# Moving the decay-matrix loads from SyncE's queue to ScalarE's, with the orders around them, in a Mamba2 block kernel

## The reference

```python
x = layernorm(x + attn(x)); x = layernorm(x + ffn(x))       # x: 2 x 512 x 512
# attn: a Mamba2 block, 128 heads of 64, state 128, 8 groups, chunks of 128 tokens
proj = einsum('bsd,ed->bse', x, in_proj_w)                  # gate | hs, B, C | dt
hBC = silu(conv1d(proj[hs, B, C], 4 taps) + conv_b)
dt = clip(softplus(dt + dt_bias), 0, 100); A_cum = cumsum(dt * -exp(A_log)) in each chunk
L = exp(segsum(dt * A))                                     # exp(A_cum[l] - A_cum[s]), l >= s
Y_diag = einsum('bzlhn,bzshn,bhzls,bzshp->bzlhp', C, B, L, hs * dt)
Y_off = C @ (state carried from the chunks before) * exp(A_cum)
g = (Y_diag + Y_off + hs * D) * silu(gate)
out = g * rsqrt(mean(g * g in each group) + eps) * norm_w
return out @ out_proj_w.T
# ffn: x @ W.T + bias plus the weighted sum of 8 low-rank products
```

## Time and profile before

| | us |
|---|---|
| median of 3 runs (lowest to highest) | 1553.58 (1553.01 to 1557.14) |
| the profiled execution's own time | 1554.98 |
| its span in the trace | 1553.1 |
| PE busy | 1522.9 (98%) |
| DVE, POOL, ACT busy | 1350.6 (87%), 1340.1 (86%), 1219.3 (79%) |

### The profile page before, as it was taken

How to read it: one execution, slowest core, us unless ns; L and a number is a source line. 1 busy time by engine, 2 the same in 40 slices (tenths; PEclk the granted TensorE clock), 3 DMA queues, 4 the chain that set the end, 5 groups by cost and what they waited for, 6 DMA issues and landing times.

```text
span 1553.1 us, 27611 instructions
## 1 busy us (share of the span) xinstructions
PE 1522.9 (98%) x8664; PEld 1260.5 (81%) x8664; DVE 1350.6 (87%) x1878; ACT 1219.3 (79%) x2360; POOL 1340.1 (86%) x1124
## 2 busy tenths in 40 slices
PE   8899999999999999999999999999999999999998
PEld 6778888878888888888888788888888888888765
DVE  6678799888989899897998979988898979989797
ACT  5888877888778887788868886888877888788863
POOL 4489989899889988899899998899988997989974
PEclk9999999999999999999999999999999999999999
DMA  3654643545345543635436454454534444363521
GB/s 114 224 181 142 191 143 120 168 143 168 111 144 173 153 147 117 193 120 158 157 118 187 127 161 143 128 182 133 171 108 162 155 141 154 123 192 121 177 89 61
DMA packets 164192, 229.06 MB, mean 147 GB/s; under 512 B 25040, under 2 KB 86480, under 8 KB 163792
## 3 DMA queue, kind: packets, MB, share of 16 engines
q1 hardware_dynamic: 163040, 227.14, 46.3%
q10 hardware_dynamic: 1008, 0.17, 0.1%
HBM read 193.14 MB, written 34.08 MB: 146 GB/s over the span
## 4 chain that ended last, share of the span: by engine, by line
PE 56%; POOL 23%; issue 10%; DVE 7%; ACT 2%; DMA 2%; SPq 0%; POOLq 0%; DVEq 0%; ACTq 0%
PE proj L665 10%; PE proj L667 10%; PE proj L666 10%; PE p_out L714 4%; PE p_out L716 4%; PE p_out L715 4%; POOL w_lo L1340 4%; POOL dh L1398 4%; PE p_st L723 3%; POOL dh L1422 3%; POOL xd_lo L1383 2%; POOL y L1443 2%; POOL xdt L1365 2%; PE p_yd L832 2%; POOL xd L1372 2%
## 5 line engine op out<-in xcount | busy, mean ns | idle before, releaser
L665 PE MATMUL proj<-x_hi,w_hi 128*128 128x512 f32 x1160 | 465.8, 402 | 7.7 <-DVE x_lo L1824 7.3
L667 PE MATMUL proj<-x_hi,w_lo 128*128 128x512 f32 x1160 | 453.9, 391 | 0.0
L666 PE MATMUL proj<-x_lo,w_hi 128*128 128x512 f32 x1160 | 453.7, 391 | 0.0
L1340 POOL TENSOR_TENSOR w_lo<-raw,w_hi 128x512 fp32r<-128x512 f32 x177 | 249.2, 1408 | 87.2 <-ACT w_hi L923 86.2
L1681 DVE SCALAR_TENSOR_TENSOR hs<-proj,uch,hs 128x511 f32<-128x511 f32 (+2 forms) x384 | 283.9, 744 | 44.1 <-ACT hs L949 38.1
L1011 ACT ACTIVATE decay<-decay,tok 128x128 f32<-128x128 f32 x1024 | 312.5, 390 | 2.5 <-DMA decay<-acum_d 2.3
L665 PEld LDWEIGHTS proj<-x_hi,w_hi 128*128 128x128 f32 x1160 | 219.6, 189 | 51.0 <-issue 9.4
L667 PEld LDWEIGHTS proj<-x_hi,w_lo 128*128 128x128 f32 x1160 | 218.7, 189 | 47.1
L666 PEld LDWEIGHTS proj<-x_lo,w_hi 128*128 128x128 f32 x1160 | 219.5, 189 | 41.7
L1443 POOL TENSOR_TENSOR y<-y,gate 128x512 f32<-128x512 f32 x128 | 193.6, 1512 | 34.2 <-DVE y L1862 25.7
L714 PE MATMUL p_out<-wo_hi,g_hi 128*128 128x512 f32 x512 | 202.5, 395 | 3.2 <-DVE g_lo L1750 2.7
(11 more groups left out here) (142 smaller groups left out, 2980.1 us busy)
## 6 DMA issues: line engine op xcount, KB each, us to landing
decay<-acum_d SPq DMA_DIRECT2D x128, 512.0 KB, 4.5
raw<-w_t SPq DMA_DIRECT2D x177, 256.0 KB, 3.6
turned_d<-x_tok_sb SPq DMA_DIRECT2D x112, 256.0 KB, 3.9
x_tok_sb<-turned_d SPq DMA_DIRECT2D x448, 64.0 KB, 1.9
eac<-eacum_d SPq DMA_DIRECT2D x192, 128.0 KB, 3.0
wo_raw<-wo_t SPq DMA_DIRECT2D x64, 256.0 KB, 4.6
hs<-x_t SPq DMA_DIRECT2D x8, 256.0 KB, 6.0
acc<-x_tok SPq DMA_DIRECT2D x8, 256.0 KB, 3.2
```

What stands on the lines that cost most here:

```text
L665: nc.tensor.matmul(dst[:], w_hi[:, ws, k, :], x_hi[:, k, cols], start=(k == 0), stop=False)
L666: nc.tensor.matmul(dst[:], w_hi[:, ws, k, :], x_lo[:, k, cols], start=False, stop=False)
L667: mm = nc.tensor.matmul(dst[:], w_lo[:, ws, k, :], x_hi[:, k, cols], start=False, stop=(k == KC - 1))
L1340: nc.gpsimd.tensor_tensor(w_lo[:, s].rearrange("p a b -> p (a b)"), raw[:, s, :], w_hi[:, s].rearrange("p a b -> p (a b)").bitcast(F32), A ...
```

## The change

124 of the 128 decay loads are issued by ACT, at fixed places between its other calls; the four of the prologue stay on SP. SP waits at two more places, before it loads a later unit's channel constants, until `skip` of the unit's last step is done. The matmul engine's order is as before. On ACT, DVE and POOL calls change places:

```diff
@@ SP: every load_decay goes (16 in a group), as in
-                load_decay(sp, g, 0, 4)
...
                 load_eac(sp, g, 0, 2)
-                load_decay(sp, g, 0, 5)
                 store_blocks(g, 0, 4)
                 load_w(g, STEP_TILES[0][4][0])
...
                 if not last:
+                    sp.wait_ge(dskip_done, carried(g, 0, 7))
                     load_channels(sp, 2 * g + 2, 0)
                     load_unit(sp, 2 * g + 2, 0)
@@ ACT, first_unit
                 exps(g, 0, 2)
                 gaps(g, 0, 3)
                 squares(g, 0, 0)
+                wo_split_hi(g, 0, (0,))
+                load_decay(act, g, 0, 4)
                 exps(g, 0, 3)
-                wo_split_hi(g, 0, (0,))
                 wo_split_hi(g, 0, (1,))
                 split_hi(g, STEP_TILES[0][1][1])
                 wo_split_hi(g, 0, (2,))
                 wo_split_hi(g, 0, (3,))
+                split_hi(g, STEP_TILES[0][2][0])
                 high_gated(step(g, 0, 0))
                 drain_proj(g, STEP_TILES[0][0][1], (0,))
-                split_hi(g, STEP_TILES[0][2][0])
                 gaps(g, 0, 4)
                 split_hi(g, STEP_TILES[0][3][0])
                 drain_proj(g, STEP_TILES[0][1][0], (0,))
                 drain_proj(g, STEP_TILES[0][1][1], (0,))
+                load_decay(act, g, 0, 5)
                 high_gated(step(g, 0, 1))
                 exps(g, 0, 4)
-                save_half(g, 0)
                 squares(g, 0, 1)
                 drain_proj(g, STEP_TILES[0][2][0], (0,))
+                save_half(g, 0)
...
@@ ACT, last_unit
                         exps(g, 1, c + 3)
+                    if c < 4:
+                        load_decay(act, g, 1, c + 4)
                     squares(g, 1, c)
@@ POOL, first_unit
-                split_lo(g, STEP_TILES[0][1][0])
-                skip(g, 0, 1)
                 decayed_tokens(g, 0, 1)
                 gate_y(g, 0, 0)
+                skip(g, 0, 1)
                 high_tokens(g, 0, 1)
                 scale_tokens(g, 0, 2)
                 low_tokens(g, 0, 1)
+                split_lo(g, STEP_TILES[0][1][0])
                 if g:
                     inv_rms(g - 1, 6)
                 split_lo(g, STEP_TILES[0][1][1])
+                add_carried(g, 0, 1)
+                decay_state(g, 0, 1)
                 split_lo(g, STEP_TILES[0][2][0])
-                decay_state(g, 0, 1)
-                add_carried(g, 0, 1)
@@ DVE, first_unit
+                state_sum(g, 0, 0)
                 turn_blocks(g, 0, 3)
                 high_tokens(g, 2)
-                state_sum(g, 0, 0)
...
-                turn_blocks(g, 0, 6)
                 square_sum(g, 0, 2)
                 tap(g, STEP_TILES[0][3][0], 0, 1)
                 tap(g, STEP_TILES[0][3][0], 0, 2)
                 tap(g, STEP_TILES[0][3][0], 0, 3)
+                turn_blocks(g, 0, 6)
```

More of the change, by code:

```diff
@@ L635, in body @@
                     load_w(g + 1, STEP_TILES[0][1][1])
+                if not last:
+                    sp.wait_ge(dskip_done, carried(g, 1, 7))
                     load_channels(sp, 2 * g + 3, 1)
@@ L1154, in first_unit @@
                 drain_proj(g, STEP_TILES[0][3][0], (1,))
+                save_half(g, 2)
                 high_gated(step(g, 0, 3))
                 squares(g, 0, 3)
+                gaps(g, 0, 7)
                 drain_proj(g, STEP_TILES[0][4][0], (0,))
-                gaps(g, 0, 7)
                 silus(g, [STEP_TILES[0][3][0]], (1,))
-                save_half(g, 2)
                 drain_proj(g, STEP_TILES[0][4][0], (1,))
@@ L1174, in first_unit @@
                 silus(g, [STEP_TILES[0][5][0]], (0,))
+                gaps(g, 1, 0)
+                load_decay(act, g, 1, 1)
                 high_gated(step(g, 0, 5))
@@ L1204, in second_unit @@
                 wo_split_hi(g, 1, (1,))
+                load_decay(act, g, 1, 4)
+                high_gated(step(g, 1, 0))
+                squares(g, 1, 0)
+                split_hi(g, STEP_TILES[1][1][1])
                 wo_split_hi(g, 1, (2,))
-                high_gated(step(g, 1, 0))
-                split_hi(g, STEP_TILES[1][1][1])
                 drain_proj(g, STEP_TILES[1][0][1], (0,))
                 save_half(g, 7)
-                squares(g, 1, 0)
                 split_hi(g, STEP_TILES[1][1][2])
@@ L1216, in second_unit @@
                 drain_proj(g, STEP_TILES[1][1][1], (0,))
-                exps(g, 1, 4)
+                load_decay(act, g, 1, 5)
                 drain_proj(g, STEP_TILES[1][1][2], (0,))
@@ L1220, in second_unit @@
                 drain_proj(g, STEP_TILES[1][1][2], (1,))
+                exps(g, 1, 4)
                 high_gated(step(g, 1, 1))
@@ L1226, in second_unit @@
                 drain_proj(g, STEP_TILES[1][2][0], (1,))
+                silus(g, [STEP_TILES[1][1][2]], (0,))
                 split_hi(g, STEP_TILES[1][4][0])
+                load_decay(act, g, 1, 6)
                 silus(g, [STEP_TILES[1][2][0]], (0,))
                 squares(g, 1, 2)
+                high_gated(step(g, 1, 2))
                 silus(g, [STEP_TILES[1][2][0]], (1,))
-                high_gated(step(g, 1, 2))
-                silus(g, [STEP_TILES[1][1][2]], (0,))
-                silus(g, [STEP_TILES[1][1][2]], (1,))
+                load_decay(act, g, 1, 7)
                 gaps(g, 1, 6)
@@ L1252, in second_unit @@
                 drain_proj(g, STEP_TILES[1][5][0], (0,))
+                drain_proj(g, STEP_TILES[1][5][0], (1,))
+                split_hi(g, STEP_TILES[1][6][0])
                 gaps(g + 1, 0, 0)
[L1254 to L1255 removed]
                 split_hi(g, STEP_TILES[1][6][1])
+                load_decay(act, g + 1, 0, 1)
                 high_gated(step(g, 1, 5))
@@ L2112, in second_unit @@
                 add_normed(g, 4)
+                turn_blocks(g + 1, 0, 2)
                 add_out(g, 6)
                 high_tokens(g + 1, 1)
+                products(g + 1, 1)
                 first_scaled(g + 1, 0)
-                products(g + 1, 1)
-                turn_blocks(g + 1, 0, 2)
                 mix(g + 1, 0, 1)
```

53 lines of the change are left out of this document (22 added, 31 removed).

## The result

The change makes the kernel slower: 1576.44 us in the median of 4 runs (1569.18 to 1581.31) against 1554.04 for the kernel before (4 runs, 1553.01 to 1557.14), a ratio of 1.0146 with a 95% interval of 1.0121 to 1.0171. The forecast was 1552.4 in a range of 1546 to 1560.

What follows compares the result with a forecast made beforehand. The matmul engine (PE), 98% busy, was taken as the bound, so only its waits count. +0.5 - 4.9 + 3.2 = -1.2 us, off the 1553.58 median, gave 1552.4 us, range 1546 to 1560.

Steps and rivals of the forecast that it cites:

- The entry of group 0: PE's start in group 0: one idle spell, ended by w_lo, instead of two; +0.5 us, ends 0 and +1.5.
- SP without the decay loads: Stores on SP no longer behind decay loads: token blocks come earlier for scale_tokens, no wait; 0, at worst about 0.4 us.
- ACT's issues: Sixteen decay-load issues per group on ACT, hidden under its activations, loads in time: 0; in full +4.1 us.
- Rival B: H0's weights come late, so project_out waits 1.3 us in seven groups: +9 us, 1561 us; chance 0.17.
- The steady groups: Moved calls remove two thirds of the 7.3 us that 13 short PE waits cost: -4.9 us, ends 0 and -7.3.
- The new wait of G10: Groups 1 to 7: PE waits for G10's later w_lo on POOL; +3.2 us, ends +1 and +5.
- The tail: Last group: the 2.7 us wait for low_gated stays, one load issue in ACT's work ahead: 0, at most +0.5 us.

Runs made afterwards that it cites:

- e4: The kernel before with all its orders, and only the 124 decay loads moved to ACT: 1566.04 us, ratio 1.0092.
- e5: The kernel before with one change, gaps(g,0,7) ahead of the drain of H2's first half: 1553.57 us, ratio 1.0002.
- e6: The kernel before with the decay loads on ACT, except those of steps (g,0,6) and (g,0,7), on SP at their old places: 1551.45 us, ratio 0.9997.
- e7: The kernel before with only the decay loads of steps (g,0,6) and (g,0,7) on ACT: 1565.32 us, ratio 1.0089.
- e13: The kernel before with all decay loads on ACT, that of step (g,0,6) earlier, ahead of gaps(g,0,5): 1554.05 us, ratio 1.0008.
- e16: The kernel before with only the loads of (g,0,6) and (g,0,7) on ACT, each 64 KB instead of 512: 1554.51 us, ratio 1.0013.
- e17: The kernel before with only the decay load of step (g,0,6) on ACT, behind exps(g,0,5): 1556.64 us, ratio 1.0033.
- e1: The changed kernel with the drain of H2's first half put back before gaps(g,0,7): 1577.49 us, ratio 1.0167.
- e2: The changed kernel with split_hi of H0 put back behind high_gated(g,0,0) and the gate's drain: 1564.47 us, ratio 1.0081.
- e8: The changed kernel's orders, but all decay loads on SP at their old places: 1567.17 us, ratio 1.0093.
- e9: The changed kernel with the decay loads of steps (g,0,6) and (g,0,7) back on SP: 1560.65 us, ratio 1.0056.
- e10: The changed kernel with the loads of (g,0,6) and (g,0,7) back on SP and split_hi of H0 put back: 1554.31 us, ratio 1.0003.
- e14: The changed kernel with the load of (g,0,6) ahead of gaps(g,0,5) and split_hi of H0 put back: 1555.74 us, ratio 1.0014.

## Why the prediction was wrong

*The entry of group 0*, +0.5: right in its way, and right in its number by luck. Measured +1.0 against the trace of before. PE idles once, for 9.64 us (8.9 forecast), and starts G10 at 84.41 (83.9 forecast):

```profile
84.41 0.77 PE L651 MATMUL proj<-x_hi,w_hi 128*128 128x512 f32 x1 [9.64 <-ACT w_hi L909]
```

The profile names `w_hi` as releaser; ACT had made it 0.9 us before, and `w_lo` on POOL came last, 0.1 us ahead. But that trace had a slow entry, with a half-clock stretch behind each of its two idle spells. At `project_out(0,0,0)` the eight traces with the order of before (before, e4 to e7, e13, e16, e17) stand from 3.2 us ahead of it to 0.4 behind, in the mean 1.7 ahead; the seven with the new order (the change, e1, e2, e8 to e10, e14) 0.3 to 1.6 behind, in the mean 0.9. So the order costs about 2.5 us, and one trace was too few for a term of half a microsecond.

*SP without the decay loads*: the step that failed. It said "I let it cost no wait", and put the late blocks of `scale_tokens` at nothing; they cost 14 us. It asked only for the order on SP, for what stands behind a decay load in the queue. It did not ask when the moved loads would be in flight. The part on ACT's issues then asked whether a load comes in time for its `gaps` (they do: none waits), and not what it does to the transfers it meets. By the Trainium skill, "DMA: Bandwidth & Descriptors", section "Issuing engines are not separate DMA queues", all issuers' transfers interleave on the same 16 engines. The runs agree with it: 512 KB beside the round trip make it 5.0 us, 64 KB 3.8 (e7, e16). The forecast quoted this rule, and priced it at 0.4 us and for group 0 alone. That there was little to spare could be read before, though not from the list of waits: none of the ten in which `scale_tokens` waited for its blocks is at step (g,0,5). But there the last block landed only 0.3 to 2.2 us ahead of the call, and `y` of step 3 stands behind it; in the changed kernel it waits 1.6 to 2.7 us in every group but group 5. Worth 13 us alone (e4, e7) and 14 with the new orders (the change against e9).

*Rival B* happened, with its place and its victim right: `project_out(g,0,0)` waits for `g_hi`'s followers in seven groups. The late partner was wrong, and the size: what came last was not the landing of `raw` (2.6 to 3.0 us after its issue, 0.1 to 0.6 us before `w_hi` began) but the slot of `w_hi`, which the projection of G10 holds until 276.6. So the wait comes in every group and doesn't hang on a landing of 3.8 us: 0.87 us each, 6.1 in all. The time at which `project_out` is due was also off: it was taken from group 0 (7.4 us behind the start of G10), where the trace of before has 6.5 in group 1. With 6.5, B would have decided from a landing of 2.9 us on, not 3.8.

*The steady groups*, -4.9: not shown. With the losses undone (e10) PE gains 2.9 us on the trace of before from group 1 to 7. But over the same stretch the traces of e5, e6, e13, e16 and e17, which keep the order of before, differ from it by -3.7 (e6) to +1.2 (e13), and e10's median is no lower than that of before.

*The new wait of G10*, +3.2: absent. PE starts G10 0.1 us behind `w_lo` in group 1 and comes no later by it than 0.05 us, in each of the seven groups; `y` took 1.3 us at its new place in all of them, where before it took 2.27 in groups 1, 3 and 7. That is the case named as the low end, and it came out below even that.

*ACT's issues*, 0: right. 0.33 us each, under an activation.

*The tail*, 0: +0.9 in the ledger.

The sum with the measured terms: +1.0 for the entry, -0.8 for what comes back, 0 for G10, +6.1 for H0, +18.9 for the late blocks and +0.9 for the tail, 26 us in the profiled execution, which is one of the two longer runs; 22 in the median. The parts of the entry and the small ones lean on a single trace of before.

## What to carry to other kernels

A transfer that moves to another queue keeps its bytes. Ask at which moment it will now be in flight, and which short transfers on a critical round trip are in flight then; here two of sixteen loads decided, and letting one of them set out some 3 us earlier undid 12 of 13 us. Follow such a trip to its last landing: the second leg was later than the first. A call that is moved ahead of another brings its own waits along: list all that it waits for, a slot's release too. And when the wait that a mended order removes turns up two steps later at the same total, its cause is further up. Last, read a small term from more than one trace of the same order of calls.

## What the runs showed of the hardware

A DMA issue on ACT, with its wait already met, costs the engine no time: 0.33 us in the queue's row, under the running activation (e4). When the 512 KB load starts within 1.5 us of the 256 KB store, on another queue, the store's successor is issued 4.2 to 6.9 us after the store (change and e4, sixteen cases), against 3.0 to 4.8 when the load goes 2.1 to 4.0 us ahead on the same queue (before, eight cases). The two overlap in other runs: 3.3 and 3.4 with the load 0.3 to 0.4 us behind (e2), 5.7 with it 2.4 us ahead on SP (e9). Over all traces, with the clock full before it, an idle spell of the matmul engine of 1.0 to 1.7 us was never followed by the lower clock (39 cases), one of 1.8 to 3.05 us was in 30 of 50, and one of 3.09 us or more in all 17; within the middle band the length doesn't tell which.
